# Diagonal attention on one core: who copies the turned rows out of PSUM, and how often the queries' rows are turned

## The chip, the cores and the metric

The kernel runs on one core of a Trainium2 chip. The metric is the device time of one execution in microseconds (us). The kernel is a whole block of layers; the change lies in one of its phases, called F here, the attention of which only the diagonal is wanted.

## What is computed

Phase F takes the layer-normed activations (2 x 2048 tokens of 128 channels) and computes

```
Q = X @ W_q + b_q ; K = X @ W_k + b_k ; V = X @ W_v + b_v     # 128 -> 128
Q = (Q * scale).reshape(n, 16, l, 8) ; K likewise ; V.reshape(n, 16, l, 8)
scores = einsum('neax,nebx->neab', Q, K)
A = softmax(scores, axis=2)                                   # over the queries
out = diagonal(A)[..., None] * V                              # then @ W_o + b_o
```

The reshape is taken straight from the (tokens, 128) array, so a head is not a slice of the channels: it is 128 consecutive tokens, each giving 16 rows of 8 numbers. One tile of 128 tokens is therefore one whole head with 2048 queries and 2048 keys, and there are 32 tiles. For each key the kernel needs the largest score over 2048 queries, the sum of the exponentials, and the key's own diagonal score. The order in which the queries are gone through doesn't matter.

## The kernel before, in words

Float32 queries and keys are split into three bf16 parts each, and the eight products of parts that count are laid side by side: a score is one contraction over 8 x 8 = 64 rows (ROWS), with bf16 operands. GpSimd writes these rows, token by token, into `d_q_rows` (`uq`) and `d_k_rows` (`uk`) in `pool_prep` (L2459 and on; L2471 the queries, L2478 the keys). TensorE turns them (L2289, transposes through the identity) into PSUM: rows of a tile are 16 slices of 128 tokens, an "eighth" being one of eight slices in a bank. One bank holds eight slices, and its 128 partitions are filled in two halves of 64, by two transposes for each slice (the loop over `r`), since TensorE's array is used as two halves of 64 contraction rows side by side.

Before the change both halves of a bank hold the same slices, for the queries and for the keys. So a tile has four banks of turned rows: k = 0 and 1 are the queries, k = 2 and 3 the keys. Each is copied out of PSUM as 128 x 1024 bf16: VectorE copies k = 0 (L2366), ScalarE k = 1, 2 and 3 (L2426), into `d_qT` and `d_kT`.

Each tile then has 32 steps (`STEPS`; step n is block n // 2 of 128 keys against half n % 2 of the queries). A step is:

- TensorE, `pe_score` (L2296 to 2306): two matmuls 64 x 128 against 64 x 512, one in each half of the array, into two banks. The bank pairs are three in rotation, so a score waits for the exponential of three steps before (L2300).
- VectorE, `dve_score` (L2372): the negated maximum over 1024 columns.
- ScalarE, `act_score` (L2434): the exponential with that maximum as bias and the sum as accumulator output, which shows as ACTIVATE and ACTIVATION_READ_ACCUMULATOR.

The other two of the eight banks are side banks, for all else: projections of the next tile ("qkv"), the four banks of turned rows of the next tile, and two small matmuls that close the tile before ("turn", "out"). They alternate, in an order written out by hand in the list `side` (L2235); who takes a side bank waits for the copy that emptied the one two entries before (`pe_side`, L2246). Since TensorE takes its instructions in order, the scores behind such a wait wait too.

`beside` (L2319) puts the side work between the steps: after each step every generator goes on to its next `yield`. So the number of yields sets the step behind which a piece of work stands. For the next tile, TensorE projects behind step 0, turns k = 0 behind steps 14 to 16, k = 1 behind 16 to 18, k = 2 behind 18 to 20 and k = 3 behind 20 to 22; VectorE copies k = 0 behind step 16; ScalarE copies k = 1, 2 and 3 behind steps 18, 20 and 22. VectorE adds the projection's biases behind step 1 and closes the tile before behind steps 1, 7, 11 and 13 (L2380, L2384, L2388, L2393). The first tile's preparation stands alone ahead of the first step, and the last tile has none beside it.

Of the kernel before, what the change touches and what calls it, by code (L numbers as in the profile page):

```python
# [7 lines left out]
F32, BF16, I32 = mybir.dt.float32, mybir.dt.bfloat16, mybir.dt.int32  # L8
# [3 lines left out]
P = 128  # L12
D = 128
BANK = 512
# [85 lines left out]
def build(nc, a, out, shape, phases=("M", "T", "C", "D", "E", "F", "E2")):  # L100
    NB, S, _ = shape
    NT = S // P
    R = NB * NT
    T, V, A, G, SP = nc.tensor, nc.vector, nc.scalar, nc.gpsimd, nc.sync
    ctx = ExitStack()
    with ctx:
# [16 lines left out]
        def sb(stack, name, shp, dt=F32):  # L123
            return stack.enter_context(nc.sbuf_tensor(name, shp, dt))
# [2054 lines left out]
        def phase_F():  # L2179
# [7 lines left out]
            with ExitStack() as st:  # L2187
# [7 lines left out]
                part = sb(st, "d_parts", [P, 3, 2 * HID], BF16)  # L2195
                uq = sb(st, "d_q_rows", [P, 2, NH, len(TERMS), HD], BF16)
                uk = sb(st, "d_k_rows", [P, 2, NH, len(TERMS), HD], BF16)
                qT = sb(st, "d_qT", [2 * ROWS, 2, NH * P], BF16)
                kT = sb(st, "d_kT", [2 * ROWS, 2, NH * P], BF16)
                dg = sb(st, "d_diag", [P, 3, NH])  # L2200
                dj = sb(st, "d_diag_terms", [P, HID])
# [13 lines left out]
                biased = signal("diag_biased", tl)  # L2215
                q_spread = signal("diag_q_spread", tl)
                k_spread = signal("diag_k_spread", tl)
                turned = signal("diag_rows_turned", [(t, k) for t in tl for k in range(4)])
                row_dve = signal("diag_rows_dve", tl)
                row_act = signal("diag_rows_act", [(t, k) for t in tl for k in range(1, 4)])  # L2220
                scored = signal("diag_scored", range(R * STEPS))
                maxed = signal("diag_max", range(R * STEPS))
                summed = signal("diag_exp", range(R * STEPS))
# [12 lines left out]
                for t in range(-1, R + 1):  # L2236
                    if t + 1 < R:
                        side.append(("qkv", t + 1))
                    if 0 <= t - 1 < R:
                        side += [("turn", t - 1), ("out", t - 1)]  # L2240
                    if t + 1 < R:
                        side += [("rows", t + 1, k) for k in range(4)]
                side_at = {u: n for n, u in enumerate(side)}
                side_bank = lambda *u: side_at[u] % 2

                def pe_side(*u):  # L2246

                    n = side_at[u]
                    if n >= 2:
                        kind, at = side[n - 2][0], side[n - 2][1:]  # L2250
                        if kind == "qkv":
                            T.wait_ge(*biased(*at))
                        elif kind == "turn":
                            T.wait_ge(*o_copied(*at))
                        elif kind == "out":
                            T.wait_ge(*added(*at))
                        elif at[1] == 0:
                            T.wait_ge(*row_dve(at[0]))
                        else:
                            T.wait_ge(*row_act(*at))  # L2260
                    return side_bank(*u)

                def sp():
# [8 lines left out]
                    leave(SP)  # L2272

                def pe_prep(t):
                    b, i, s = t // NT, t % NT, t % 2
                    bk = pe_side("qkv", t)
                    T.matmul(bank(bk)[:, 0:3 * HID], chans[:, b, PAD + i * P:PAD + (i + 1) * P], w[:, :],
                             start=True, stop=True).then_inc(*projected.up(t))
                    for _ in range(14):
                        yield  # L2280
                    T.wait_ge(*q_spread(t))
                    for k in range(4):
                        u = uk if k >= 2 else uq
                        if k == 2:
                            T.wait_ge(*k_spread(t))
                        rows = bank(pe_side("rows", t, k)).bitcast(BF16)
                        for q in range(8):
                            for r in range(2):
                                last = T.transpose(rows[ROWS * r:ROWS * r + ROWS, q * P:(q + 1) * P],  # L2289
                                                   u[:, s, 8 * (k % 2) + q].rearrange("p n x -> p (n x)"), identb[:, :])  # L2290
                            if q == 7:
                                last.then_inc(*turned.up(t, k))
                            if q % 3 == 2:
                                yield

                def pe_score(t, n):  # L2296
                    s, jb, hf = t % 2, n // 2, n % 2
                    at = t * STEPS + n
                    if at >= 3:
                        T.wait_ge(*summed(at - 3))  # L2300
                    for jj in range(2):
                        c = 2 * hf + jj
                        half = slice(ROWS * jj, ROWS * jj + ROWS)
                        last = T.matmul(bank(2 + 2 * (at % 3) + jj), kT[half, s, jb * P:(jb + 1) * P], qT[half, s, c * BANK:(c + 1) * BANK],  # L2304
                                        start=True, stop=True)
                    last.then_inc(*scored.up(at))

# [22 lines left out]
                def pe():  # L2330
                    enter(T)
                    for b in range(NB):
                        T.wait_ge(*ln_out("F", b))
                        for g in range(4):
                            pe_turn_group("F", b, g, 4 * b + g, norm)
                    leave(T)
                    enter(T)
                    for _ in pe_prep(0):
                        pass

                    def score(t, n):
                        if n == 0:
                            T.wait_ge(*row_act(t, 3))
                            T.wait_ge(*row_dve(t))
                        pe_score(t, n)
                    beside(pe_prep, pe_close, score)
                    leave(T)

                def dve_prep(t):
# [9 lines left out]
                    V.tensor_tensor(vf[:, t % 3, :], bank(bk)[:, 2 * HID:3 * HID], bias[:, 2, :], ALU.add).then_inc(*biased.up(t))  # L2359
                    for _ in range(15):  # L2360
                        yield
                    V.wait_ge(*turned(t, 0))
                    if t >= 2:
                        V.wait_ge(*scored((t - 1) * STEPS - 1))
                    rows = bank(side_bank("rows", t, 0)).bitcast(BF16)
                    V.tensor_copy(qT[:, s, 0:8 * P], rows).then_inc(*row_dve.up(t))  # L2366
                    yield

                def dve_score(t, n):
                    at = t * STEPS + n  # L2370
# [44 lines left out]

                def act_prep(t):
                    s = t % 2
                    for k in range(1, 4):
                        for _ in range(18 if k == 1 else 2):
                            yield  # L2420
                        A.wait_ge(*turned(t, k))
                        if t >= 2:
                            A.wait_ge(*scored((t - 1) * STEPS - 1))
                        dst = kT if k >= 2 else qT
                        rows = bank(side_bank("rows", t, k)).bitcast(BF16)
                        A.copy(dst[:, s, (k % 2) * 8 * P:(k % 2 + 1) * 8 * P], rows).then_inc(*row_act.up(t, k))  # L2426
                    yield

                def act_score(t, n):
# [29 lines left out]
                def pool_prep(t):  # L2459
# [5 lines left out]
                    gstep(G.tensor_copy(part[:, 1, :], rest[:, :]))  # L2465
                    gstep(G.tensor_tensor(part[:, 2, :], rest[:, :], part[:, 1, :], ALU.subtract))
                    if t >= 2:
                        G.wait_ge(*turned(t - 2, 3))
                    for g in range(3):
                        rows = uq[:, s, :, of_q[g], :]  # L2470
                        last = G.tensor_copy(rows, wide(heads(part[:, g, 0:HID]), 2, rows.shape[2]))  # L2471
# [86 lines left out]
```

## Time and profile before

| what | us |
|---|---|
| median of 3 runs (lowest, highest) | 4824.35 (4823.6, 4824.75) |
| the profiled execution, its own time | 4827.53 |
| its span | 4826.2 |
| the steps of phase F in it | from 2693.4 to 4018.5 |

TensorE was busy for 3784.1 us of the span, VectorE for 3457.4, ScalarE for 2956.7 and GpSimd for 838.6. The profiled execution is 3.2 us longer than the median, and its span 1.3 us shorter than its own time. In the profile PE is TensorE's matmuls, PEld its weight loads, DVE is VectorE, ACT ScalarE, POOL GpSimd; an idle time is given with what ended it, and L with a number is a line of the kernel.

### The profile page before, as it was taken

What the parts mean: (1) busy time and instruction counts of PE and PEld (TensorE: products, weight loads), DVE (VectorE), ACT (ScalarE), POOL (GpSimd) and SP (SyncE); (2) the same over time, 40 slices, a digit from 0 to 9 for tenths busy, and PEclk for the clock granted to TensorE, in tenths of its full rate; (3) what the DMA queues carried; (4) which work ended last, traced back from release to release, by engine and by line L of the source; (5) the groups of instructions that cost most, each with busy time, mean ns of one, the idle gap of its engine ahead of it and who ended that gap; (6) DMA issues with size and microseconds to landing.
All of it is one profiled execution on the core that took longest, in us unless ns stands there. A gap on an engine that the chain in (4) does not pass through costs nothing.

```text
span 4826.2 us, 78862 instructions
## 1 busy us (share of the span) xinstructions
PE 3784.1 (78%) x31382; PEld 2009.6 (42%) x31382; DVE 3457.4 (72%) x5239; ACT 2956.7 (61%) x4913; POOL 838.6 (17%) x1094
## 2 busy tenths in 40 slices
PE   6888558858869996899999566666666664899998
PEld 4666333222234442567666211111111111567666
DVE  6888666476451003778787899999999996778787
ACT  3444126626623333566665699999999995566665
POOL 2444210000036762000000111111111110000000
PEclk8999759969979998999999555555555556999999
DMA  1000000000022210000000000000000000000000
GB/s 42 1 1 1 1 3 1 1 0 1 1 72 36 44 26 17 8 15 2 11 2 5 2 1 1 1 1 1 1 1 1 1 1 18 8 15 2 11 2 19
DMA packets 49884, 45.20 MB, mean 9 GB/s; under 512 B 21203, under 2 KB 34910, under 8 KB 49502
## 3 DMA queue, kind: packets, MB, share of 16 engines
q1 hardware_dynamic: 49518, 40.16, 4.0%
q8 instruction: 250, 4.10, 0.4%
q14 instruction: 116, 0.95, 0.1%
HBM read 29.52 MB, written 2.23 MB: 7 GB/s over the span
## 4 chain that ended last, share of the span: by engine, by line
PE 47%; DVE 29%; issue 11%; ACT 10%; POOL 2%; DMA 1%; SPq 1%; DVEq 0%; ACTq 0%; POOLq 0%
DVE d_negmax L2372 11%; PE psum L1872 7%; PE psum L1901 6%; PE psum L1887 5%; DVE f_m_E L2017 5%; PE psum L1507 5%; PE psum L1530 4%; ACT d_junk L2434 4%; PE psum L1124 2%; PE psum L1113 2%; PE psum L1098 2%; ACT wl_p L1345 2%; DVE f_pT_E L2036 1%; DVE wl_negmax L1250 1%; PE psum L498 1%
## 5 line engine op out<-in xcount | busy, mean ns | idle before, releaser
L2372 DVE TENSOR_REDUCE d_negmax<-psum 128x1 f32<-128x1024 f32 x1024 | 1184.6, 1215 | 101.4 <-PE psum L2304 101.4
L2434 ACT ACTIVATE d_junk<-psum,d_negmax 128x1024 bf16<-128x1024 f32 x1024 | 1137.8, 1128 | 75.7 <-DVE d_negmax L2372 68.0
L2304 PE MATMUL psum<-d_qT,d_kT 64*128 64x512 bf16 x2048 | 605.5, 600 | 440.6 <-ACT d_junk L2434 424.2
L2123 ACT ACTIVATE hidden<-psum,f_nm_E 128x1024 f32<-128x1024 f32 x512 | 566.5, 1113 | 141.7 <-DVE f_nm_E L2020 141.5
L2017 DVE TENSOR_REDUCE f_m_E<-psum 128x1 f32<-128x1024 f32 x512 | 602.3, 1218 | 47.7 <-PE psum L1872 47.5
L1872 PE MATMUL psum<-f_k_E,f_q_swapped_E 64*128 64x512 f32 x1024 | 526.9, 624 | 6.6 <-ACT hidden L2123 6.6
L1872 PE MATMUL psum<-f_k_E,f_q_E 64*128 64x512 f32 x1024 | 526.9, 624 | 2.8 <-DMA f_q_swapped_E<-f_q_E 1.4
L1901 PE MATMUL psum<-f_pT_E,f_v_E 128*64 128x128 f32 x8192 | 503.7, 276 | 2.5 <-DVE residual L2047 2.5
L2130 ACT COPY f_pT_E<-psum 128x512 f32<-128x512 f32 x512 | 300.1, 586 | 319.8 <-PE psum L1887 319.7
L2036 DVE COPY f_pT_E<-psum 128x512 f32<-128x512 f32 x512 | 351.7, 687 | 157.4 <-PE psum L1887 146.9
L2304 PEld LDWEIGHTS psum<-d_qT,d_kT 64*128 64x128 bf16 x2048 | 106.0, 101 | 857.9 <-ACT d_junk L2434 805.5
L1901 PEld LDWEIGHTS psum<-f_pT_E,f_v_E 128*64 128x64 f32 x8192 | 442.5, 137 | 20.1 <-ACT f_pT_E L2130 2.8
L1887 PEld LDWEIGHTS psum<-ident,hidden 64*128 64x128 f32 x8192 | 317.4, 140 | 234.8 <-issue 185.3
L1664 POOL TENSOR_TENSOR moe_h<-moe_h,moe_gates_on_all 128x512 f32<-128x512 f32 x256 | 322.8, 1294 | 494.2 <-DMA moe_gates_on_all<-moe_gate_spill 364.6
L1250 DVE TENSOR_REDUCE wl_negmax<-psum 128x1 f32<-128x1024 f32 x256 | 305.5, 1222 | 142.4 <-PE psum L1098 138.4
L1887 PE MATMUL psum<-ident,hidden 64*128 64x64 f32 x8192 | 358.6, 227 | 47.8 <-DVE f_pT_E L2036 44.8
L1649 ACT ACTIVATE moe_h<-psum,moe_b 128x512 f32<-128x512 f32 x256 | 175.4, 687 | 271.8 <-PE psum L1530 271.8
L1345 ACT ACTIVATE wl_p<-psum 128x1024 f32<-128x1024 f32 x256 | 253.2, 1026 | 110.8 <-PE psum L1113 110.4
L1507 PE MATMUL psum<-moe_h,moe_w 128*128 128x512 f32 x512 | 232.2, 597 | 8.9 <-POOL moe_h L1664 8.9
L1530 PE MATMUL psum<-normed_channels,moe_w 128*128 128x512 f32 x512 | 235.4, 604 | 0.0
L1594 DVE COPY moe_yT<-psum 128x512 f32<-128x512 f32 x8 | 5.5, 692 | 312.3 <-PE psum L1507 312.3
L2434 ACT ACTIVATION_READ_ACCUMULATOR d_junk<-psum,d_negmax 128x1 f32 x1024 | 216.6, 212 | 0.0
(313 smaller groups left out, 5246.5 us busy)
## 6 DMA issues: line engine op xcount, KB each, us to landing
moe_gates_on_all<-moe_gate_spill SPq DMA_DIRECT2D x8, 2048.0 KB, 15.8
f_q_swapped_E<-f_q_E SPq DMA_DIRECT2D x64, 128.0 KB, 2.4
moe_w<-in_moe_w SPq DMA_DIRECT2D x8, 256.0 KB, 4.0
out<-residual SPq DMA_DIRECT2D x1, 2048.0 KB, 8.7
residual<-in_hidden_states SPq DMA_DIRECT2D x2, 768.0 KB, 7.4
residual<-in_hidden_states SPq DMA_DIRECT2D x2, 256.0 KB, 3.4
m_taps<-in_m_conv SPq DMA_DIRECT2D x4, 128.0 KB
level_sums<-in_c_sums SPq DMA_DIRECT2D x1, 512.0 KB
```

What stands on the lines that cost most here:

```text
L1250: V.tensor_reduce(negm[:, i, h:h + 1], two(slot(*step)), X, ALU.max, negate=True).then_inc(*maxed.up(b, h, i))
L1507: last = T.matmul(acc, w2[:, e * FT + f, :], hbuf[:, n % 2, f, :], start=False, stop=(e == E_ - 1 and f == FT - 1))
L1530: T.matmul(bank(f), w1[:, e, f * P:(f + 1) * P], chans[:, b, PAD + g * BANK:PAD + (g + 1) * BANK], start=True, stop=True).then_inc(*made.u ...
L1872: last = T.matmul(bank(2 * f + jj), (q if jj == h else q_sw)[half, w, qs], k2[half, w, h, f, :], start=True, stop=True)
L1887: last = T.transpose(bank(4 + r)[:, q * 64:(q + 1) * 64], pb[half, u % 2, kt * P:(kt + 1) * P], ident[half, half])
L1901: last = T.matmul(bank(6)[64 * h:64 * h + 64, 0:P], vt[:, n % 2, kt, h, :], pT[:, (2 * t + h) % 4, kt, :], start=(kt == 0), stop=(kt == NT ...
L2017: last = V.tensor_reduce(m2[:, u % 4, f:f + 1], two(2 * f), X, ALU.max)
L2036: V.tensor_copy(pT[:, u % 4, 8 * g:8 * g + 8, 64:P], bank(5).rearrange("p (q n) -> p q n", n=64)).then_inc(*pT_dve.up(u, g))
L2123: A.activation(pb[:, u % 2, f * 2 * BANK:(f + 1) * 2 * BANK], two(2 * f), ACT.Exp, bias=nm[:, u % 4:u % 4 + 1], scale=SC, accum_out=rs[:, ...
L2304: last = T.matmul(bank(2 + 2 * (at % 3) + jj), kT[half, s, jb * P:(jb + 1) * P], qT[half, s, c * BANK:(c + 1) * BANK], start=True, stop=True)
L2372: V.tensor_reduce(mh[:, t % 2, n // 2, n % 2:n % 2 + 1], two(2 + 2 * (at % 3)), X, ALU.max, negate=True).then_inc(*maxed.up(at))
L2434: A.activation(junk[:, at % 3, :], two(2 + 2 * (at % 3)), ACT.Exp, bias=mh[:, t % 2, n // 2, n % 2:n % 2 + 1], accum_out=sh[:, t % 2, n // ...
```

## The change

The queries' rows are turned once: bank k = 0 gets slices 0 to 7 in its lower half and slices 8 to 15 in its upper half, and `d_qT` is half as wide. A score's two matmuls read the same columns, each in its own half of the partitions. So there are three banks of turned rows in place of four: k = 0 the queries, k = 1 and 2 the keys. VectorE copies k = 0 (behind step 16) and k = 1 (behind step 19), ScalarE copies k = 2 (behind step 20). TensorE turns k = 1 behind steps 16 to 18 and k = 2 behind steps 18 to 20.

```diff
-                qT = sb(st, "d_qT", [2 * ROWS, 2, NH * P], BF16)
+                qT = sb(st, "d_qT", [2 * ROWS, 2, NH * P // 2], BF16)
...
-                turned = signal("diag_rows_turned", [(t, k) for t in tl for k in range(4)])
-                row_dve = signal("diag_rows_dve", tl)
-                row_act = signal("diag_rows_act", [(t, k) for t in tl for k in range(1, 4)])
+                turned = signal("diag_rows_turned", [(t, k) for t in tl for k in range(3)])
+                row_dve = signal("diag_rows_dve", [(t, k) for t in tl for k in range(2)])
+                row_act = signal("diag_rows_act", tl)
...
-                        side += [("rows", t + 1, k) for k in range(4)]
+                        side += [("rows", t + 1, k) for k in range(3)]
...
-                        elif at[1] == 0:
-                            T.wait_ge(*row_dve(at[0]))
+                        elif at[1] < 2:
+                            T.wait_ge(*row_dve(*at))
                         else:
-                            T.wait_ge(*row_act(*at))
+                            T.wait_ge(*row_act(at[0]))
...
-                    for k in range(4):
-                        u = uk if k >= 2 else uq
-                        if k == 2:
+                    for k in range(3):
+                        u = uk if k else uq
+                        if k == 1:
                             T.wait_ge(*k_spread(t))
                         rows = bank(pe_side("rows", t, k)).bitcast(BF16)
                         for q in range(8):
                             for r in range(2):
+                                eighth = 8 * (k - 1 if k else r) + q
                                 last = T.transpose(rows[ROWS * r:ROWS * r + ROWS, q * P:(q + 1) * P],
-                                                   u[:, s, 8 * (k % 2) + q].rearrange("p n x -> p (n x)"), identb[:, :])
+                                                   u[:, s, eighth].rearrange("p n x -> p (n x)"), identb[:, :])
...
-                        c = 2 * hf + jj
                         half = slice(ROWS * jj, ROWS * jj + ROWS)
-                        last = T.matmul(bank(2 + 2 * (at % 3) + jj), kT[half, s, jb * P:(jb + 1) * P], qT[half, s, c * BANK:(c + 1) * BANK],
+                        last = T.matmul(bank(2 + 2 * (at % 3) + jj), kT[half, s, jb * P:(jb + 1) * P], qT[half, s, hf * BANK:(hf + 1) * BANK],
                                         start=True, stop=True)
...
-                            T.wait_ge(*row_act(t, 3))
-                            T.wait_ge(*row_dve(t))
+                            T.wait_ge(*row_act(t))
+                            T.wait_ge(*row_dve(t, 1))
...
-                    V.wait_ge(*turned(t, 0))
-                    if t >= 2:
-                        V.wait_ge(*scored((t - 1) * STEPS - 1))
-                    rows = bank(side_bank("rows", t, 0)).bitcast(BF16)
-                    V.tensor_copy(qT[:, s, 0:8 * P], rows).then_inc(*row_dve.up(t))
-                    yield
+                    for k, dst in enumerate((qT[:, s, :], kT[:, s, 0:8 * P])):
+                        V.wait_ge(*turned(t, k))
+                        if t >= 2:
+                            V.wait_ge(*scored((t - 1) * STEPS - 1))
+                        V.tensor_copy(dst, bank(side_bank("rows", t, k)).bitcast(BF16)).then_inc(*row_dve.up(t, k))
+                        for _ in range(3):
+                            yield
...
-                    for k in range(1, 4):
-                        for _ in range(18 if k == 1 else 2):
-                            yield
-                        A.wait_ge(*turned(t, k))
-                        if t >= 2:
-                            A.wait_ge(*scored((t - 1) * STEPS - 1))
-                        dst = kT if k >= 2 else qT
-                        rows = bank(side_bank("rows", t, k)).bitcast(BF16)
-                        A.copy(dst[:, s, (k % 2) * 8 * P:(k % 2 + 1) * 8 * P], rows).then_inc(*row_act.up(t, k))
+                    for _ in range(20):
+                        yield
+                    A.wait_ge(*turned(t, 2))
+                    if t >= 2:
+                        A.wait_ge(*scored((t - 1) * STEPS - 1))
+                    A.copy(kT[:, s, 8 * P:16 * P], bank(side_bank("rows", t, 2)).bitcast(BF16)).then_inc(*row_act.up(t))
                     yield
...
-                        G.wait_ge(*turned(t - 2, 3))
+                        G.wait_ge(*turned(t - 2, 2))
```

## Rows read from the trace of the kernel before

**Rows 1.** Page, costliest groups: line engine op, out<-in, count | busy us, mean ns | idle before

```profile
L2372 DVE TENSOR_REDUCE d_negmax<-psum 128x1 f32<-128x1024 f32 x1024 | 1184.6, 1215 | 101.4 <-PE psum L2304 101.4
L2434 ACT ACTIVATE d_junk<-psum,d_negmax 128x1024 bf16<-128x1024 f32 x1024 | 1137.8, 1128 | 75.7 <-DVE d_negmax L2372 68.0
```

**Rows 2.** Stretches: us, busy (x) PE, PEld, DVE, ACT, POOL, PEclk, DMA, GB/s

```profile
2693.40:4018.50 1325.10, 828.69 (x4187) 238.59 (x4187) 1225.96 (x1242) 1249.34 (x2204) 247.21 (x651) 0.52 0.00 1
3000.06:3041.56 41.50, 26.35 (x135) 7.62 (x135) 38.37 (x40) 39.09 (x71) 7.97 (x22) 0.50 0.00 1
```

**Rows 3.** Timeline of VectorE, one tile: start us, us, what, xcount [idle before]

```profile
3000.62 1.22 DVE L2372 TENSOR_REDUCE d_negmax<-psum 128x1 f32<-128x1024 f32 x1 [0.30 <-PE psum L2304]
...
3001.96 3.48 DVE L2372 TENSOR_REDUCE d_negmax<-psum 128x1 f32<-128x1024 f32 x3
3005.36 0.68 DVE L2366 COPY d_qT<-psum 128x1024 bf16<-128x1024 bf16 x1
3005.95 4.61 DVE L2372 TENSOR_REDUCE d_negmax<-psum 128x1 f32<-128x1024 f32 x4
3011.61 3.49 DVE L2372 TENSOR_REDUCE d_negmax<-psum 128x1 f32<-128x1024 f32 x3 [1.05 <-PE psum L2304]
3015.36 2.36 DVE L2372 TENSOR_REDUCE d_negmax<-psum 128x1 f32<-128x1024 f32 x2 [0.27 <-PE psum L2304]
3018.47 8.01 DVE L2372 TENSOR_REDUCE d_negmax<-psum 128x1 f32<-128x1024 f32 x7 [0.75 <-PE psum L2304]
3027.25 1.23 DVE L2372 TENSOR_REDUCE d_negmax<-psum 128x1 f32<-128x1024 f32 x1 [0.77 <-PE psum L2304]
```

**Rows 4.** Timeline of ScalarE, the same tile, steps 18 to 22

```profile
3008.33 1.11 ACT L2434 ACTIVATE d_junk<-psum,d_negmax 128x1024 bf16<-128x1024 f32 x1
...
3009.44 1.00 ACT L2426 COPY d_qT<-psum 128x1024 bf16<-128x1024 bf16 x1
3010.33 1.13 ACT L2434 ACTIVATE d_junk<-psum,d_negmax 128x1024 bf16<-128x1024 f32 x1
...
3011.43 1.12 ACT L2434 ACTIVATE d_junk<-psum,d_negmax 128x1024 bf16<-128x1024 f32 x1
...
3012.52 1.03 ACT L2426 COPY d_kT<-psum 128x1024 bf16<-128x1024 bf16 x1
3013.41 1.15 ACT L2434 ACTIVATE d_junk<-psum,d_negmax 128x1024 bf16<-128x1024 f32 x1
...
3014.51 1.15 ACT L2434 ACTIVATE d_junk<-psum,d_negmax 128x1024 bf16<-128x1024 f32 x1
...
3015.61 1.05 ACT L2426 COPY d_kT<-psum 128x1024 bf16<-128x1024 bf16 x1
```

**Rows 5.** Timeline of TensorE, the same tile, behind steps 18 to 24

```profile
3006.35 0.53 PE L2289 MATMUL psum<-ident_bf,d_k_rows 128*64 128x128 bf16 x6
...
3010.49 0.53 PE L2289 MATMUL psum<-ident_bf,d_k_rows 128*64 128x128 bf16 x6 [1.07 <-ACT d_qT L2426]
...
3014.71 0.61 PE L2304 MATMUL psum<-d_qT,d_kT 64*128 64x512 bf16 x2 [1.25 <-ACT d_junk L2434]
```

**Rows 6.** Waits, 2700 to 4015 us: who waited for whom: us in total, times, longest

```profile
PE psum L2289 <- ACT d_qT L2426: 35.1, 31, 1.4
```

**Rows 7.** Timelines: GpSimd writes the keys' rows, and TensorE turns behind step 16

```profile
2999.41 1.54 POOL L2478 COPY d_k_rows<-d_parts 128x384 bf16<-128x384 bf16 x3
...
3003.68 0.75 PE L2289 MATMUL psum<-ident_bf,d_q_rows 128*64 128x128 bf16 x10
```

**Rows 8.** Timeline of all engines, the first tile's preparation

```profile
2689.22 0.69 DVE L2366 COPY d_qT<-psum 128x1024 bf16<-128x1024 bf16 x1 [5.29 <-PE psum L2289]
...
2690.06 2.22 PE L2289 MATMUL psum<-ident_bf,d_k_rows 128*64 128x128 bf16 x32
...
2692.32 1.01 ACT L2426 COPY d_kT<-psum 128x1024 bf16<-128x1024 bf16 x1
...
2693.39 0.61 PE L2304 MATMUL psum<-d_qT,d_kT 64*128 64x512 bf16 x2 [1.11 <-ACT d_kT L2426]
```

## The prediction

> **What bounds the kernel now.** I read first which engine idles least where the change lies. On the page the maximum (L2372) and the exponential (L2434) are the two costliest groups, 1024 of each, and each engine idles only 101.4 and 75.7 us ahead of them [rows 1]. Over all steps of phase F, 1325.1 us, VectorE is busy for 1226 us and ScalarE for 1249; TensorE with 829 us has room [rows 2]. So two engines take turns, and busy time alone doesn't say which of them sets the pace. TensorE's granted clock there is 0.52 of full speed, so nearly always the lower level, 1.2 GHz [rows 2].
>
> Next the timeline of VectorE over one tile, the view that decides. The tile from 3000.06 is 41.50 us long [rows 2]; the same pattern stands in the others I looked at, to 0.1 us. Maxima that follow one another start every (4.61 - 1.22) / 3 = 1.13 us; the records overlap by 0.09. Five gaps are in the tile: 0.30 before step 13, 1.05 before step 21, 0.27 before step 24, 0.75 before step 26, 0.77 before step 1 of the next [rows 3]. Through the seven maxima from step 26 on there is no gap: there VectorE is the bound, and ScalarE keeps up, since its exponentials can start every 1.10 us (3010.33 to 3011.43, 3013.41 to 3014.51) [rows 3, 4].
>
> The three gaps before 21, 24 and 26 come from ScalarE's three copies of turned rows. A copy puts the next exponential off by 0.89 us beyond its step: 3012.52 to 3013.41 [rows 4]. The bank pair of exponential 21, started at 3013.41, is scored again at 3014.71, 1.30 us later, and the maximum 24 starts at 3015.36, another 0.65 later [rows 3 to 5]. The largest gap has a second cause: behind step 20 TensorE wants the side bank that ScalarE's copy behind step 18 empties, and stands for 1.07 us with score 21 queued behind it [rows 5]; 31 such waits, 35.1 us in all [rows 6].
>
> **The change, part by part.** (1) *Gaps that go.* With the overlap of 0.09 each, the three gaps hold up VectorE by 1.05 + 0.27 + 0.75 + 3 x 0.09 = 2.34 us a tile.
>
> (2) *VectorE's second copy.* The same form as its first, which moves the next maximum from 3005.36 to 3005.95, so 0.59, say 0.60 us [rows 3]. It stands on the bounding engine, and nothing hides it. The floor is that pitch; the ceiling is what a copy of this form costs between two instructions of ScalarE, 0.89 [rows 4]. I take 0.60: it is the same instruction in the same surroundings, three steps later. The row shows that the next instruction starts 0.09 us before the copy's record ends [rows 3]. The Trainium skill, VectorE: DVE Perf Modes, section "The DRAIN you can't avoid", says otherwise: the next operation starts only after a flush of about the operation's length less 266 ns. By it the copy would cost 0.68 + 0.41 = 1.09 us as an estimate, and the gain of a tile would be 0.60 us; the trace disagrees here, so the row is used.
>
> (3) *The gap that stays.* ScalarE still copies once, behind step 20. I follow the tile on from 3005.95 by the pitches above. Maxima 17, 18 and 19 start at 3005.95, 3007.08 and 3008.21 as now; where 20 stands now, at 3005.95 + 3 x 1.13 = 3009.34, comes VectorE's new copy, and maximum 20 at 3009.94, with its end (1.22 later) at 3011.16. Exponential 20 follows at 3011.18, the copy at 3012.28, exponential 21 at 3012.28 + 0.89 = 3013.17. Score 24 can start 1.30 later, at 3014.47, and maximum 24 another 0.65 later, at 3015.12. VectorE could have been there at 3009.94 + 4 x 1.13 = 3014.46, so it is held up by 0.66 us. Maxima 25 and 26 wait no more: exponential 23 starts at 3013.17 + 2 x 1.10 = 3015.37, which allows maximum 26 at 3017.32, and VectorE gets there at 3015.12 + 2 x 1.13 = 3017.38. In the trace of before, maximum 26 stands at 3018.47 [rows 3]. The gain is 1.09 a tile; the terms give the same, 2.34 - 0.66 - 0.60 = 1.08.
>
> (4) *TensorE.* 16 transposes a tile go. Ten of them take 0.75 us [rows 7], so some 1.2 us of an engine that has 15 us free in the tile [rows 2]: nothing by itself. What goes with them is the wait for ScalarE's first copy, counted in (1). Two waits are left to look at. The third bank (keys, behind step 18) waits for VectorE's copy of the queries, as k = 2 does now: that copy is over at 3005.36 + 0.68 = 3006.04, and the transposes that need it run at 3006.35, with no idle time [rows 3, 5]. The keys' rows are now wanted behind step 16 in place of 18; GpSimd has written them by 2999.41 + 1.54 = 3000.95, and the turning behind step 16 starts at 3003.68 [rows 7]. Cover 2.7 us, nothing late. The gaps of 0.30 and 0.77 are not touched: no turned rows stand there. The score matmuls keep their form; no DMA is added or moved, and GpSimd only waits for another number of the same signal.
>
> (5) *The first tile's preparation*, ahead of all steps: four banks in a row, the last two turned in 2.22 us, the last copy from 2692.32, and the first score at 2693.39 [rows 8]. One bank less is worth at most its 1.1 us, at least nothing, as VectorE and ScalarE now copy side by side but the keys' rows are waited for; I take 0.6, the middle.
>
> Sum: 31 tiles have a preparation beside them, 31 x 1.09 = 33.8, and 0.6 before: 34.4 us. The profiled execution of 4827.5 us would become 4793.1; it lies 3.2 us above the median of 4824.35, so the median becomes 4790.
>
> **Rivals.** *A, the forecast*, as above, with 0.85 to 1.35 us a tile: 4782 to 4797.
>
> *B, less gain.* ScalarE's copy holds up VectorE twice, as now, with the 0.27 before 24 kept beside the 0.75 of a lone copy (1.20 with overlaps): 2.34 - 1.20 - 0.60 = 0.54 a tile, 17 us, 4807. For it: ScalarE gains on VectorE by no more than 0.03 us a step, so what one copy puts it behind can come back at the pair's next turn. Against: by the working of (3) nothing is late after maximum 24, but the margin at maximum 26 is only 0.06 us.
>
> *C, a dearer copy.* VectorE's copy costs what ScalarE's does, 0.89: 1.69 - 0.89 = 0.80 a tile, 25 us, 4799. This is the side on which the page's rule in (2) lies; by its 0.60 a tile it would be 4805. Against: 31 copies of that form on VectorE stand in the trace, and the one in the rows moves the next maximum by 0.60.
>
> *D, more gain.* The gap of (3) goes too, because VectorE's copy at step 19 lets TensorE get ahead: 2.34 - 0.60 = 1.74 a tile, 54 us, 4770. Against: the three bank pairs are in rotation whatever is moved, and ScalarE's delay comes after VectorE's, not beside it.
>
> *E, slower.* VectorE becomes the bound with its gaps kept: the gaps before 21, 24 and 26 stand three or two steps apart, as the rotation of three pairs would also have it. If the rotation made them and not the copies, they stay, and the added copy is paid in full: 31 x 0.60 = 19 us, 4843. It decides from the point where the gaps that stay beyond the 0.77 and 0.30 exceed 2.34 - 0.60 = 1.74 a tile. Against: seven maxima from step 26 on run with no gap in the same rotation, and TensorE's 1.07 names ScalarE's copy.
>
> *F, it doesn't do what it says:* the gaps are ScalarE's only in part, 1.74 of them stay, and nothing changes: 4824.
>
> **How the numbers follow.** A change of 0.2%, 9.6 us, is about what a measurement of this kernel can tell from none. A has 0.68, B 0.11, C 0.03, D 0.08, E 0.04, F 0.06; A to D are all faster. Faster 0.90, within 0.2% 0.06, slower 0.04. The range, 4775 to 4808, takes in A whole with B and C and stops short of D's point; the ceiling of (2) is worth 31 x 0.29 = 9 us and the bounds of (5) half a us each way, both inside.
>
> **What would show it.** VectorE should have two copies of 0.68 us in a tile, behind steps 16 and 19, and between step 13 and step 1 of the next tile one gap of about 0.56 before maximum 24 in place of 1.05, 0.27 and 0.75. ScalarE's copies should number 32 in place of 96, TensorE should wait for no ScalarE copy of rows, and the tile should be 40.4 us long. VectorE's busy time should be up by about 20 us with its gaps down by 47. I am wrong if a gap stands before 21 (TensorE held by another copy), or if a second one stands before 26 or 27 (B), or if the phases around F, whose clock could shift, move by more than some us.

## The result, and the profile after

The changed kernel took 4789.69 us (median of 4 runs, 4785.25 to 4793.63) against 4823.98 (median of 4, 4821.05 to 4824.75): a ratio of 0.993, with a 95% interval of 0.9913 to 0.9947. The profiled execution took 4793.63 us (its span is 4792.3) against 4827.53: 33.9 us less. On another chip, beside the variants below, the changed kernel came to 4784.87 (4783.41 to 4790.39) against 4823.45, a ratio of 0.9922 (0.9908 to 0.9935).

The page's costliest groups, after (line engine op, out<-in, count | busy us, mean ns | idle before); they answer to [rows 1]:

```profile
L2374 DVE TENSOR_REDUCE d_negmax<-psum 128x1 f32<-128x1024 f32 x1024 | 1181.6, 1216 | 52.1 <-PE psum L2305 52.1
L2433 ACT ACTIVATE d_junk<-psum,d_negmax 128x1024 bf16<-128x1024 f32 x1024 | 1135.0, 1117 | 91.8 <-DVE d_negmax L2374 84.0
```

VectorE's idle time ahead of its maxima has halved, from 101.4 to 52.1 us; ScalarE's has grown, from 75.7 to 91.8. Of the two engines that took turns at the pace, VectorE is now the one that mostly sets it, going by these idle times.

Busy time of one tile, after (columns as in [rows 2], which has the tile of before):

```profile
2844.79:2885.20 40.41, 24.80 (x119) 6.85 (x117) 38.79 (x40) 37.48 (x68) 7.93 (x21) 0.54 0.00 1
```

The tile takes 40.41 us in place of 41.50. ScalarE works 1.6 us less in it, VectorE 0.4 more, TensorE 1.6 less, still at the lower clock nearly all the time (granted 0.54).

The timeline of VectorE over the same part of a tile as in [rows 3], after:

```profile
2754.60 0.68 DVE L2367 COPY d_qT<-psum 128x1024 bf16<-128x1024 bf16 x1
2755.20 3.48 DVE L2374 TENSOR_REDUCE d_negmax<-psum 128x1 f32<-128x1024 f32 x3
2758.59 0.68 DVE L2367 COPY d_kT<-psum 128x1024 bf16<-128x1024 bf16 x1
2759.19 4.61 DVE L2374 TENSOR_REDUCE d_negmax<-psum 128x1 f32<-128x1024 f32 x4
2764.36 10.28 DVE L2374 TENSOR_REDUCE d_negmax<-psum 128x1 f32<-128x1024 f32 x9 [0.56 <-PE psum L2305]
2775.40 1.23 DVE L2374 TENSOR_REDUCE d_negmax<-psum 128x1 f32<-128x1024 f32 x1 [0.76 <-PE psum L2305]
```

There are two copies, each of which moves the next maximum by 0.60 us (2754.60 to 2755.20, 2758.59 to 2759.19). The gaps of 1.05, 0.27 and 0.75 are gone; a single one of 0.56 stands before maximum 24. The gap before step 1 is what it was (0.76, before 0.77). The list of waits no longer has TensorE waiting for a copy of ScalarE between the steps: the 35.1 us of [rows 6] are gone.

The timeline of ScalarE around its one copy left, in a later tile:

```profile
2841.26 1.11 ACT L2433 ACTIVATE d_junk<-psum,d_negmax 128x1024 bf16<-128x1024 f32 x1 [0.53 <-DVE d_negmax L2374]
...
2842.36 1.00 ACT L2425 COPY d_kT<-psum 128x1024 bf16<-128x1024 bf16 x1
2843.26 1.13 ACT L2433 ACTIVATE d_junk<-psum,d_negmax 128x1024 bf16<-128x1024 f32 x1
```

Two things stand one behind the other here. Before exponential 20, ScalarE waits 0.53 us, since VectorE had been copying; then it copies for 0.90 us itself, with VectorE working. Each engine's copy holds up the other at another time. The experiments come back to this.

The first maximum of phase F starts at 2693.45 us, before at 2694.04, with the phases ahead the same to 0.1 us up to the first projection. From the first maximum to the last it is 1287.7 us against 1322.0: 34.3 us less. With the earlier start the last maximum comes 34.9 us earlier; what follows it took 811.2 us in place of 810.2, which leaves the 33.9 of the profiled executions.

### The profile page after: what moved, and what is told of

It reads as the page before. It is cut to its first block, busy times and chain, and to the rows that moved or that the text cites. A ratio compares the mean times of both kernels' runs of the same rounds, so it can differ in the third digit from the quotient of the medians.

```text
span 4792.3 us, 77776 instructions
## 1 busy us (share of the span) xinstructions
PE 3737.3 (78%) x30870; PEld 1983.9 (41%) x30870; DVE 3467.6 (72%) x5271; ACT 2903.1 (61%) x4849; POOL 836.7 (17%) x1094
## 4 chain that ended last, share of the span: by engine, by line
PE 47%; DVE 32%; issue 10%; ACT 8%; POOL 1%; DMA 1%; SPq 1%; DVEq 0%; POOLq 0%; ACTq 0%
DVE d_negmax L2374 13%; PE psum L1872 7%; PE psum L1901 6%; PE psum L1887 5%; DVE f_m_E L2017 5%; PE psum L1507 5%; PE psum L1530 4%; ACT d_junk L2433 4%; PE psum L1124 2%; PE psum L1113 2%; ACT wl_p L1345 2%; PE psum L1098 2%; DVE wl_negmax L1250 1%; DVE f_pT_E L2036 1%; PE psum L498 1%
## 5 line engine op out<-in xcount | busy, mean ns | idle before, releaser
L2374 DVE TENSOR_REDUCE d_negmax<-psum 128x1 f32<-128x1024 f32 x1024 | 1181.6, 1216 | 52.1 <-PE psum L2305 52.1
L2433 ACT ACTIVATE d_junk<-psum,d_negmax 128x1024 bf16<-128x1024 f32 x1024 | 1135.0, 1117 | 91.8 <-DVE d_negmax L2374 84.0
L2433 ACT ACTIVATION_READ_ACCUMULATOR d_junk<-psum,d_negmax 128x1 f32 x1024 | 205.6, 201 | 0.0
```

The lines of the kernel that those rows point to most:

```text
L2374: V.tensor_reduce(mh[:, t % 2, n // 2, n % 2:n % 2 + 1], two(2 + 2 * (at % 3)), X, ALU.max, negate=True).then_inc(*maxed.up(at))
L2433: A.activation(junk[:, at % 3, :], two(2 + 2 * (at % 3)), ACT.Exp, bias=mh[:, t % 2, n // 2, n % 2:n % 2 + 1], accum_out=sh[:, t % 2, n // ...
```

## The experiments

The theory is the working of the prediction: VectorE's maxima start every 1.13 us and ScalarE's exponentials every 1.10; a copy puts VectorE off by 0.60 and ScalarE by 0.89; three bank pairs in rotation carry ScalarE's delay back to VectorE. The rivals are that only the move of a copy matters, that VectorE alone is the bound and ScalarE's copies are hidden, and that fewer transposes are themselves a gain. Since executions of one kernel lie up to 10 us apart, each run is read by its tile length first and its time second. Each ratio is against the kernel before on the same chip.

### Which part of the change brings the time

One run keeps the single turning of the queries but leaves both banks of keys to ScalarE:

```diff
-                    for k, dst in enumerate((qT[:, s, :], kT[:, s, 0:8 * P])):
-                        V.wait_ge(*turned(t, k))
+                    V.wait_ge(*turned(t, 0))
...
+                    for k in (1, 2):
+                        for _ in range(18 if k == 1 else 2):
+                            yield
+                        A.wait_ge(*turned(t, k))
...
+                        A.copy(kT[:, s, (k - 1) * 8 * P:k * 8 * P], bank(side_bank("rows", t, k)).bitcast(BF16)).then_inc(*row_act.up(t, k))
```

> Three banks as in the changed kernel, queries turned once, but VectorE copies only k = 0 and ScalarE both banks of keys (behind steps 18 and 20). My theory, by the same pitches: VectorE's second copy (0.60) goes, two gaps come, about 0.6 before maximum 22 and about 0.75 before maximum 24, and maximum 26 stands 0.85 us earlier than before the change: tile 40.65, time about 4797. So turning the queries once alone would bring some 27 of the 34 us. Rival, the move of copies from ScalarE to VectorE is what pays: time within 10 us of the 4824 of before, tile over 41.2.

Measured: 4796.76 us (4794.75 to 4799.0), ratio 0.9944 (0.9931 to 0.9958). VectorE's timeline, from before maximum 22 of one tile to the same place in the next:

```profile
3003.43 2.36 DVE L2372 TENSOR_REDUCE d_negmax<-psum 128x1 f32<-128x1024 f32 x2 [0.56 <-PE psum L2305]
3006.54 10.27 DVE L2372 TENSOR_REDUCE d_negmax<-psum 128x1 f32<-128x1024 f32 x9 [0.75 <-PE psum L2305]
...
3044.08 1.23 DVE L2372 TENSOR_REDUCE d_negmax<-psum 128x1 f32<-128x1024 f32 x1 [0.56 <-PE psum L2305]
```

The tile is 3044.08 - 3003.43 = 40.65 us, with the two gaps where they were expected. Turning once, without the move, takes 0.85 us off a tile, and the rival that only the move pays is out.

The other run does the opposite. It starts from the kernel before, with four banks and the queries turned twice, and only moves a copy:

```diff
-                    V.wait_ge(*turned(t, 0))
...
-                    V.tensor_copy(qT[:, s, 0:8 * P], rows).then_inc(*row_dve.up(t))
-                    yield
+                    for k in range(2):
+                        V.wait_ge(*turned(t, k))
...
+                        V.tensor_copy(qT[:, s, k * 8 * P:(k + 1) * 8 * P], rows).then_inc(*row_dve.up(t, k))
+                        for _ in range(3):
+                            yield
...
-                    for k in range(1, 4):
-                        for _ in range(18 if k == 1 else 2):
+                    for k in range(2, 4):
+                        for _ in range(20 if k == 2 else 2):
```

> Four banks as before the change, the queries still turned twice, but VectorE copies both banks of queries (behind steps 16 and 19) and ScalarE both banks of keys (behind 20 and 22). My theory: the fourth bank, wanted by TensorE behind step 20, now waits some 0.5 us for VectorE's second copy in place of 1.07 for ScalarE's; the gap before maximum 21 is at most 0.15, that before 24 about 0.56, that before 26 about 0.75; with VectorE's added 0.60 maximum 26 stands only 0.2 us earlier than before: tile 41.25, time about 4817. Rival, moving pays and turning once is free: within 10 us of 4790.

Measured: 4819.08 us (4814.56 to 4822.28), ratio 0.9988 (0.9979 to 0.9997). TensorE behind step 20, then VectorE:

```profile
3003.15 0.42 PE L2289 MATMUL psum<-ident_bf,d_k_rows 128*64 128x128 bf16 x4
3004.23 0.53 PE L2289 MATMUL psum<-ident_bf,d_k_rows 128*64 128x128 bf16 x6 [0.66 <-DVE d_qT L2367]
```

```profile
2999.51 0.68 DVE L2367 COPY d_qT<-psum 128x1024 bf16<-128x1024 bf16 x1
...
3009.26 2.36 DVE L2374 TENSOR_REDUCE d_negmax<-psum 128x1 f32<-128x1024 f32 x2 [0.43 <-PE psum L2304]
3012.37 8.01 DVE L2374 TENSOR_REDUCE d_negmax<-psum 128x1 f32<-128x1024 f32 x7 [0.75 <-PE psum L2304]
...
3040.76 0.68 DVE L2367 COPY d_qT<-psum 128x1024 bf16<-128x1024 bf16 x1
```

The tile is 3040.76 - 2999.51 = 41.25 us, so the move alone takes 0.25 off. TensorE still stands behind step 20, now for VectorE's second copy (0.66 us, expected 0.5). That wait costs VectorE little: maximum 21 starts 0.12 us late (at 3005.34, 1.25 after maximum 20 in place of 1.13), and the gap before 24 is smaller by as much, 0.43 rather than 0.56. What the fourth bank does cost is the gap of 0.75 before maximum 26, behind ScalarE's copy of it: 0.84 us with the overlap. The two parts add up in either order: 41.50 - 40.65 = 0.85 and 40.65 - 40.41 = 0.24; 41.50 - 41.25 = 0.25 and 41.25 - 40.41 = 0.84. So 27 of the 34 us come from the bank that is no longer turned and copied, and 7 from giving VectorE a copy. From the first maximum to the last the profiled executions say the same: 1322.0 us before, 1295.5 turned once only, 1314.3 moved only, 1287.7 with both. The medians split less evenly (4796.8 - 4784.9 = 12 us for the move in one order, 4823.5 - 4819.1 = 4 in the other), by the scatter of whole executions.

### What TensorE's fewer transposes are worth

```diff
+                                for _ in range(2 if k == 2 else 1):
-                                last = T.transpose(rows[ROWS * r:ROWS * r + ROWS, q * P:(q + 1) * P],
+                                    last = T.transpose(rows[ROWS * r:ROWS * r + ROWS, q * P:(q + 1) * P],
```

> The changed kernel with each of the 16 transposes of the third bank done twice, so that TensorE turns 64 slices a tile as before the change and no copy is added. My theory: TensorE has the time; score 21 is ready at just about the moment VectorE wants it, so the tile grows by at most 0.1 us, the time by at most 3 us. Rival, the fewer transposes are a part of the gain: a new gap before maximum 20 or 21 of 0.3 us or more, 10 us or more.

Measured: 4785.64 us (4785.06 to 4789.71), and a tile of 40.40 us (VectorE's first copies at 3032.89 and 3073.29), with the same gaps of 0.56, 0.76 and 0.30 as the changed kernel. It is the changed kernel's time to within its scatter, with the extra transposes behind steps 18 to 20; TensorE's granted clock over the steps was 0.56 in this run, 0.53 in the changed kernel. The transposes cost nothing that shows; the copy and the waits that went with them did.

### What a copy costs on each engine

First the split: VectorE takes all three.

```diff
-                    for k, dst in enumerate((qT[:, s, :], kT[:, s, 0:8 * P])):
+                    for k, dst in enumerate((qT[:, s, :], kT[:, s, 0:8 * P], kT[:, s, 8 * P:16 * P])):
...
-                    A.copy(kT[:, s, 8 * P:16 * P], bank(side_bank("rows", t, 2)).bitcast(BF16)).then_inc(*row_act.up(t))
```

> The changed kernel with VectorE copying all three banks (behind steps 16, 19 and 22) and ScalarE none. My theory: the gap of 0.56 before maximum 24 goes (0.65 with the overlap), another copy of 0.60 comes; the tile stays within 0.1 of 40.41 and the time within 3 us of the changed kernel's (about 4789). Rival, ScalarE was the bound: the tile falls by 0.89 us, 4762. Rival, VectorE was the bound and its gap is the rotation's: tile 41.0, 4808.

Measured: 4786.55 us (4784.79 to 4790.21), tile 3076.89 - 3036.54 = 40.35 us. VectorE's third copy and the ten maxima from 23 on:

```profile
3044.53 0.68 DVE L2363 COPY d_kT<-psum 128x1024 bf16<-128x1024 bf16 x1
3045.12 11.40 DVE L2370 TENSOR_REDUCE d_negmax<-psum 128x1 f32<-128x1024 f32 x10
```

The gap before maximum 24 is gone (0.65 with the overlap) and VectorE's third copy (0.60) has taken its place. Neither engine is "the" bound that one could unload onto the other.

Then one copy more, on VectorE and on ScalarE, both behind step 26, where neither has other work. In both, one copy goes to a tile that nothing reads:

```diff
+                    V.tensor_copy(dead[:, s, :], bank(side_bank("rows", t, 1)).bitcast(BF16))
+                    for _ in range(7):
+                        yield
+                    V.tensor_copy(kT[:, s, 0:8 * P], bank(side_bank("rows", t, 1)).bitcast(BF16)).then_inc(*row_dve.up(t, 1))
```

> The changed kernel with one more copy of 128 x 1024 on VectorE in each tile, behind step 26 where neither engine has other work (the copy behind 19 goes to a tile that nothing reads, the real one stands behind 26). My theory: it costs its pitch, 0.60 us a tile, 31 x 0.60 = 19 us: tile 41.0, about 4809. Rival (the flush of the skill's page): 1.09 us a tile, 34 us, 4824. Rival, ScalarE sets the pace there and hides it: under 5 us.

Measured: 4809.05 us (4804.52 to 4810.32), ratio 0.9964 (0.9951 to 0.9977), tile 3041.49 - 3000.48 = 41.01 us: 0.60 more than the changed kernel. VectorE's row of the copy and those around it:

```profile
3010.24 3.49 DVE L2380 TENSOR_REDUCE d_negmax<-psum 128x1 f32<-128x1024 f32 x3 [0.56 <-PE psum L2306]
3013.65 0.68 DVE L2374 COPY d_kT<-psum 128x1024 bf16<-128x1024 bf16 x1
3014.24 6.87 DVE L2380 TENSOR_REDUCE d_negmax<-psum 128x1 f32<-128x1024 f32 x6
```

From the copy's start to that of the next maximum it is 0.59, and 0.60 on the tile, less than its record of 0.68; no other gap has changed. The rival that ScalarE hides the copy is out. The flush of the Trainium skill, VectorE: DVE Perf Modes, section "The DRAIN you can't avoid", would make it 1.09 us and 4824 as an estimate; the trace rules that out for a copy out of PSUM between maxima. The same section of the Trainium skill adds that a next operation that is not held back until the one before has finished starts earlier. The prediction left that out; the 0.60 agrees with it.

```diff
+                    A.copy(dead[:, s, :], bank(side_bank("rows", t, 2)).bitcast(BF16))
+                    for _ in range(6):
+                        yield
                     A.copy(kT[:, s, 8 * P:16 * P], bank(side_bank("rows", t, 2)).bitcast(BF16)).then_inc(*row_act.up(t))
```

> The changed kernel with one more copy of 128 x 1024 on ScalarE in each tile, behind step 26 (the copy behind 20 goes to a tile that nothing reads, the real one stands behind 26). My theory: exponential 27 is put off by 0.89, the pair of exponential 27 is wanted again by maximum 30, so a gap of about 0.56 (0.65 with the overlap) comes before maximum 30: tile 41.06, about 4810, as dear as a copy on VectorE although VectorE is the busier engine. Rival, VectorE alone is the bound and hides it: tile 40.41, no change. Rival, the copy costs in full: 0.89 a tile, 4817.

Measured: 4817.06 us, ratio 0.9981 (0.9972 to 0.999), 11 of its 12 runs between 4811.8 and 4820.2, with a median of 4816.6. One took 8613 us; it is left out of the ratio, and I can't say why it took that long. The tile is 3044.47 - 3003.21 = 41.26 us. VectorE's timeline:

```profile
3012.97 6.88 DVE L2375 TENSOR_REDUCE d_negmax<-psum 128x1 f32<-128x1024 f32 x6 [0.56 <-PE psum L2306]
3020.45 3.50 DVE L2375 TENSOR_REDUCE d_negmax<-psum 128x1 f32<-128x1024 f32 x3 [0.61 <-PE psum L2306]
3024.85 1.23 DVE L2375 TENSOR_REDUCE d_negmax<-psum 128x1 f32<-128x1024 f32 x1 [0.90 <-PE psum L2306]
```

This is a miss: I had said 41.06 and 4810. The gap before maximum 30 came as forecast (0.61, for 0.56), but the gap before step 1, 0.76 in the changed kernel, grew to 0.90. Together 0.61 + 0.09 + 0.14 = 0.84 us, which is the 0.85 of the tile. By the length it looks like the rival "in full, 0.89", but the timeline shows two gaps: ScalarE gains on VectorE by 0.03 us a step, seven steps are too few to make up what it lacks, and the projection's hold-up of TensorE finds it still late. TensorE's timeline bears this out. Score 0, the last one ahead of the projection, waits 0.58 us for an exponential and goes at 3022.08, 1.87 us before VectorE has done what it had (3020.45 + 3.50 = 3023.95); in the changed kernel, run again, it goes 2.02 us before (3014.14 and 3016.16), so it is 0.15 us late. A copy of ScalarE is the dearer one at this place, 0.85 against 0.60, though VectorE is the busier engine (38.90 us of this tile against 38.21).

### Where the copies stand

If each engine's copy holds up the other at another time, the delays of two copies behind the same step should overlap. The smallest such edit moves VectorE's second copy by one step:

```diff
-                        for _ in range(3):
+                        for _ in range(4):
                             yield
```

> The changed kernel with VectorE's second copy one step later, behind step 20, the same step behind which ScalarE copies. My theory (pitches of VectorE 1.13, of ScalarE 1.10; a copy puts VectorE off by 0.60 and ScalarE by 0.89; three bank pairs in rotation): with exponential 20 starting at E, VectorE's maximum 21 starts at E + 0.51 and would reach maximum 24 at E + 3.90; ScalarE's exponential 21 starts at E + 1.99, which allows maximum 24 at E + 3.94. So the gap of 0.56 before maximum 24 falls to under 0.1, the tile from 40.41 to 39.8 us, the time from 4790 to about 4771. Rival, VectorE alone is the bound and its gap is the rotation's: the copy costs 0.60 wherever it stands, the gap stays, 4790. Second rival: both engines' copies read PSUM at the same time and slow one another: copies longer than 0.68 and 1.01 us, time above 4790.

Measured: 4770.32 us (4766.79 to 4776.73), ratio 0.9894 (0.9879 to 0.9909). It was run again beside the next two:

> The variant with VectorE's and ScalarE's copies both behind step 20 once more, on the chip of these two: tile 39.80, 4767 to 4777.

Measured: 4773.15 us (4768.38 to 4776.5), ratio 0.9894 (0.9879 to 0.9909). VectorE's timeline of the first of the two:

```profile
3022.00 1.22 DVE L2374 TENSOR_REDUCE d_negmax<-psum 128x1 f32<-128x1024 f32 x1 [0.30 <-PE psum L2305]
3026.74 0.68 DVE L2367 COPY d_qT<-psum 128x1024 bf16<-128x1024 bf16 x1
3031.86 0.68 DVE L2367 COPY d_kT<-psum 128x1024 bf16<-128x1024 bf16 x1
3032.46 13.71 DVE L2374 TENSOR_REDUCE d_negmax<-psum 128x1 f32<-128x1024 f32 x12
3046.93 1.23 DVE L2374 TENSOR_REDUCE d_negmax<-psum 128x1 f32<-128x1024 f32 x1 [0.76 <-PE psum L2305]
...
3066.54 0.68 DVE L2367 COPY d_qT<-psum 128x1024 bf16<-128x1024 bf16 x1
```

No gap is left between step 13 and step 1 of the next tile. The tile is 3066.54 - 3026.74 = 39.80 us, and VectorE's copies last 0.68 us as before. The first rival, by which the gap stays, is out. The two copies are not at the same time: VectorE's is over at 3032.54, and ScalarE, which first does exponential 20, copies from 3033.08 to 3033.97, while VectorE is still at the maximum 21 that its own copy made late. So the second rival, copies that slow one another, was not put to the test. One changed number brings half as much again as the whole change.

Then the same thought with two copies on ScalarE. VectorE is back to one, of the queries, now behind step 19, and ScalarE copies the first half of the keys behind that same step. The second half isn't used before step 16 of its own tile, so its copy can stand where ScalarE waits anyway ("in cover"): behind step 0, ahead of the maximum that the projection holds up.

```diff
+                        if k == 2:
+                            for _ in range(3):
+                                yield
...
+                        if n == STEPS // 2:
+                            T.wait_ge(*row_act(t, 2))
...
+                def act_prep(t):
+                    if t >= 2:
+                        act_rows(t - 1, 2)
+                    for _ in range(19):
+                        yield
+                    act_rows(t, 1)
```

> From the variant with both copies behind step 20: VectorE copies only the queries' bank, behind step 19; ScalarE copies the first half of the keys behind step 19 too, and the second half, which no score needs before step 16 of its own tile, behind step 0 of that tile, where ScalarE waits 0.78 us for a maximum held up by the projection. TensorE turns the third bank behind steps 21 to 23. My theory: a copy on ScalarE is free where VectorE is late already (0.89 against 0.60 behind step 19 with some 0.2 to 0.3 of play; 0.89 against 0.86 behind step 0), so VectorE's second copy of 0.60 goes and nothing comes for it: tile 39.2 us against 39.80, time about 4752. Rival, what ScalarE takes on it has to give back somewhere, since it works 39 us a tile in the kernel before: tile 39.8 or more, 4770 or more.

Measured: 4753.02 us (4749.57 to 4756.47), ratio 0.9849 (0.9836 to 0.9863). Its VectorE timeline, then ScalarE's:

```profile
3003.21 1.22 DVE L2379 TENSOR_REDUCE d_negmax<-psum 128x1 f32<-128x1024 f32 x1 [0.76 <-PE psum L2308]
3018.09 1.23 DVE L2379 TENSOR_REDUCE d_negmax<-psum 128x1 f32<-128x1024 f32 x1 [0.30 <-PE psum L2308]
3026.22 0.68 DVE L2373 COPY d_qT<-psum 128x1024 bf16<-128x1024 bf16 x1
3026.82 14.84 DVE L2379 TENSOR_REDUCE d_negmax<-psum 128x1 f32<-128x1024 f32 x13
3042.42 1.23 DVE L2379 TENSOR_REDUCE d_negmax<-psum 128x1 f32<-128x1024 f32 x1 [0.76 <-PE psum L2308]
```

```profile
3002.49 1.11 ACT L2446 ACTIVATE d_junk<-psum,d_negmax 128x1024 bf16<-128x1024 f32 x1
...
3003.59 1.00 ACT L2427 COPY d_kT<-psum 128x1024 bf16<-128x1024 bf16 x1
3004.48 1.13 ACT L2446 ACTIVATE d_junk<-psum,d_negmax 128x1024 bf16<-128x1024 f32 x1
```

The tile is 3042.42 - 3003.21 = 39.21 us, 2.29 less than before the change. ScalarE copies from 3003.59 to 3004.48 while VectorE has the late maximum 1 (3003.21 to 3004.43), and its exponential follows on that maximum at once. What it copies there costs nothing that shows: the gap before maximum 1 is 0.76 as before, and no other has come.

The control has the same copies and transposes, with ScalarE's second copy behind step 25 in place of step 0 (the edit is shown against the run before it):

```diff
                 def act_prep(t):
-                    if t >= 2:
-                        act_rows(t - 1, 2)
...
-                    if t in (0, R - 1):
-                        act_rows(t, 2)
+                    act_rows(t, 2)
```

> The same as the run before it in every copy and every transpose, but ScalarE's second copy stands behind step 25 of the tile before, where VectorE is not late. My theory: a gap of about 0.56 before maximum 29, and as in the run with the extra ScalarE copy something more of the gap before step 1, since ScalarE catches up by only 0.03 us a step: together 0.65 to 0.85 a tile, tile 39.85 to 40.05, time 4771 to 4778. Rival, place doesn't matter: as the run before it.

Measured: 4775.38 us (4774.9 to 4779.98), ratio 0.9899 (0.9884 to 0.9914). VectorE's timeline:

```profile
3004.61 4.62 DVE L2379 TENSOR_REDUCE d_negmax<-psum 128x1 f32<-128x1024 f32 x4 [0.61 <-PE psum L2308]
3010.11 1.23 DVE L2379 TENSOR_REDUCE d_negmax<-psum 128x1 f32<-128x1024 f32 x1 [0.88 <-PE psum L2308]
...
3044.64 2.36 DVE L2379 TENSOR_REDUCE d_negmax<-psum 128x1 f32<-128x1024 f32 x2 [0.61 <-PE psum L2308]
```

The tile is 40.03 us: 0.82 more than the run before it for the same work, by the same two gaps as with the extra copy (0.61, and 0.88 in place of 0.76). The rival that place doesn't matter is out.

### The changed kernel again

> The changed kernel once more, on the same chip as its variants, since its four runs lie 8 us apart. Theory and rivals alike: tile 40.41, time 4785 to 4794.

Measured: 4784.87 us (4783.41 to 4790.39); tile 3040.51 - 3000.11 = 40.40 us.

| kernel | copies VectorE, ScalarE | tile us | time us | ratio |
|---|---|---|---|---|
| before | 1, 3 | 41.50 | 4824 | 1 |
| copy moved only | 2, 2 | 41.25 | 4819.1 | 0.9988 |
| turned once only | 1, 2 | 40.65 | 4796.8 | 0.9944 |
| the change | 2, 1 | 40.41 | 4784.9, 4789.7 | 0.9922, 0.993 |
| the change, idle transposes | 2, 1 | 40.40 | 4785.6 | 0.9921 |
| all on VectorE | 3, 0 | 40.35 | 4786.6 | 0.9921 |
| the change, one more on VectorE | 3, 1 | 41.01 | 4809.1 | 0.9964 |
| the change, one more on ScalarE | 2, 2 | 41.26 | 4817.1 | 0.9981 |
| the change, copies behind one step | 2, 1 | 39.80 | 4770.3, 4773.2 | 0.9894 |
| ScalarE's two in cover | 1, 2 | 39.21 | 4753.0 | 0.9849 |
| the same out of cover | 1, 2 | 40.03 | 4775.4 | 0.9899 |

## Why the prediction was right

**The bound.** Two engines in turn, seen from VectorE's gaps: right. The three gaps were ScalarE's copies, and for the first of them TensorE's wait for one, and not the rotation's. They went with the copies (the change, all on VectorE) and one came at the forecast step with a new copy (the extra copy on ScalarE). That settles rival E.

**Gaps that go, 2.34, and the copy, 0.60.** The three gaps went whole, and the copy came out to the hundredth: 0.60 twice in the timeline of after, and 0.60 a tile for one more in the extra-copy run. One sign was off: VectorE's busy time was to be up by about 20 us, and over the steps it is up by 12.7 (1225.96 to 1238.70), 0.42 in the tile shown (38.37 to 38.79). A copy adds its 0.68 less an overlap of 0.09, and where two of the three gaps have closed, neighbouring records overlap again by 0.09 each: 0.59 - 0.18 = 0.41 as an estimate. The idle time fell by 49.3 us, where 47 was forecast. The forecast of the time uses neither. Rival C, the dearer copy, is out.

**The gap that stays, 0.66.** It is 0.56 with the overlap of 0.09, before maximum 24 and nowhere else. The margin of 0.06 at maximum 26 held, so rival B's second gap did not come; but what B said of ScalarE's slow catching up is real, and showed where a copy stands closer to the next hold-up (0.85 a tile with the extra copy, 0.82 in the control). Rival D's step was wrong for this edit and right for its neighbour: the gap does go when VectorE is late at the same step as ScalarE, not one step earlier.

**TensorE.** The covers named held: no wait for VectorE's copy behind step 18, none for GpSimd's rows behind 16, and 16 transposes a tile cost nothing (the idle transposes). The prediction did not say what part of the gain belongs to the fourth bank. With four banks the wait behind step 20 stays, 0.66 us for VectorE's copy, but it only makes maximum 21 late by 0.12; the 0.84 us of the fourth bank is the gap before maximum 26, behind ScalarE's last copy.

**The first tile's preparation**, 0.6: the first maximum starts 0.59 earlier. The 0.6 was the middle between nothing and 1.1, so that it fits to the hundredth is luck.

**The sum**, 33.8 + 0.6 = 34.4 us. Like against like, the 33.8 came out as 34.3, from the first maximum to the last, and the 0.6 as 0.59: 34.9 us. That the profiled executions differ by 33.9 comes from the 1.0 us more that the rest of the kernel took behind phase F, which no run explains and which is within the "some us" that the prediction allowed. That the median fell within 1 us of 4790 is partly luck: on the second chip it was 5 us lower.

## What to carry to other kernels

Where two engines hand each other tiles through few buffers, price a side task not by its length alone but by when it stands: beside a moment in which its engine would wait anyway it is free, one step off the other engine's copy it can cost in full (0.61 of 0.60 for VectorE's second), and on the less busy engine it can cost more than on the busier one. So look first for side work that both engines have, and put it behind the same step; here placement alone, with the same copies on the same engines, took 1.44 us off a tile (turned once only, 40.65, to two in cover, 39.21), and dropping a quarter of the copies 0.85. Work that need not be done (a bank turned and copied twice) is worth what it costs the engines that hand over, and nothing that showed for the engine with time to spare.

## What was not expected of the hardware

The scatter between executions of one kernel, up to 10 us, comes from outside phase F as far as the profiled executions show it. In all thirteen of them, which have the same phases ahead of F, the first maximum started anywhere from 2687.5 to 2694.0 us, and the first tile's preparation accounts for only 0.6 of that. From the first maximum to the last it was 1287.7 and 1287.8 us in the two of the changed kernel, and 1269.2 both times in the two of the variant with the copies behind one step, whose first maxima lie 3.0 us apart. What varies in the phases ahead was not looked into.
